# A delta-rule stage on one core: a lag of its own for every stage of a head, a new order of work, and a factor without its masked copy

## The chip, the core and the metric

One core of one Trainium2 chip runs the whole kernel in one launch. Five instruction streams run beside each other and meet at semaphores: TensorE (PE), VectorE (DVE), ScalarE (ACT), GpSimd (POOL) and SyncE (SP), which issues the DMAs. The metric is the device time of one launch in microseconds (us).

## The reference

Two transformer layers over 2 sequences of 512 tokens with 256 channels. The change lies in the first attention, a gated delta rule with 32 value heads of 128 x 128 state, two to each of 16 key heads:

```python
mixed = silu(causal_conv1d(x @ w_qkv, conv_w))   # 4 taps
q, k, v = split(mixed);  q, k = l2norm(q), l2norm(k)
beta = sigmoid(x @ w_b)
g = -exp(A_log) * softplus(x @ w_a + dt_bias)
for t in range(512):                             # per head
    St = St * exp(g_t)
    delta = (v_t - k_t @ St) * beta_t
    St = St + outer(k_t, delta)
    o_t = (q_t * 128**-0.5) @ St
core = rmsnorm(o) * norm_weight * silu(x @ w_z)
x = x + core @ w_out
```

After it come a routed feed-forward layer, a causal attention and a second routed feed-forward layer; these are the same before and after the change.

## The kernel before, in words

`phase_delta` handles one key head at a time (HK = 16 heads; here "head" means that with its two value heads and the two sequences, U = 4 units). The 512 tokens are cut into CH = 4 chunks of 128. Everything is fp32.

A head goes through two groups of stages. The first is the projection: `conv0` to `conv7` (PE), their eviction `conv_r` (ACT, two passes, L807 and L808), the three remaining taps `tapa`, `tapb`, `tapc` (DVE, L943), `silu` (ACT, L819), transposes `queries`, `keys`, `vals`, the gate (`gate` on PE, `gate_r` on ACT), the decay matrices (`row` loads on SP, `gap` on POOL at L733 and L735, `dexp` on ACT at L861), the Gram products (`gram`, `mt`, `at`), the scalars (`scal` copies a head's scalars into `hs`, `nscal` on POOL works out factors such as `nck`), and the factor `nl` (DVE, L990). For `nl`, POOL first writes `cm`, a strictly lower mask times the column `nck` (L741), and DVE multiplies the Gram block by it. The 16 x 16 diagonal blocks of `nl` are then sent through DRAM into lanes (`gath`, `gathr`), inverted there by small DVE operations (`lane0` to `lane12`), transposed (`yl`) and sent back (`putx`, `puty`, `scatx`, `scaty`) into X16 and Y.

The second group (`TURN_STAGES`) merges the inverted blocks to 32, 64 and 128 (`v`, `m`, `y`, `a`, `xa`, `xb`; the number is 2 x level + half), and then walks over the chunks: `recall`, `rhs`, `solve`, `dl`, `ds`, `update`, `st` carry the state, `recallq`, `qs`, `output`, `o` make the output, and `square`, `factor`, `oz`, `corev`, `core`, `core_r`, `project`, `project_r` norm, gate and project it into x.

The order is written out by hand: `WINDOW` is one list of some 230 names, and each engine takes from it, in this order, those stages that are its own. One window handles the second group of head H and the first group of head H + 1. In front stands `PRO` (the first group of head 0 alone), behind 15 windows `LAST` (the second group of head 15 alone). So each stage is either one window ahead or not. At the start of a window SP runs `head`: it waits until PE has filled everything of the window before and loads the weights of head H + 2 (L600) and the output weights of head H + 1 (L603); then come the `row` loads (L636).

Two PSUM banks `pp` are shared by `conv`, `queries`, `keys`, `vals`, `gate`, `core` and `project` in turn: a use waits until the one two before it has been evicted (`fill`, `taken`, `filled`). Lines that the prediction's steps touch: PE `v` L1223 and L1228, `y` L1246 and L1251, `solve` L1283, `update` L1303, `project` L1323, `gate` L1192; ACT `m` of levels 1 and 2 L880 (writes dr_V), `a` of level 1 L886 and L887 (writes dr_Y); DVE `xa` L1089 and L1090, `at` L984, `rhs` L1109; POOL `ds` L760, `am` L748, `oz` L772, `yz` L753 and L754; SP `putx` L653, `scaty` L669, `scatx` L663.

Of the kernel before, what the change touches and what calls it, by code (L numbers as in the profile page):

```python
# [333 lines left out]
WINDOW = """  # L334
conv1 row0 scal conv_r1 row1 conv0 gap0 conv_r0 tapa1 tapb1 tapc1 tapa0 conv3 tapb0 gap1 v0 silu1 conv_r3 m0 row2
tapc0 silu0 conv2 conv_r2 tapa3 dexp0 y0 tapb3 queries0 a0 qsq0 tapc3 xa0 v1 tapa2 v2 dexp1 m2 conv5 y2 row3 m1 y1
yz tapb2 tapc2 silu3 a2 silu2 v4 keys0 xb0 gram0 conv_r5 m4 queries1 keys_r0 ksq0 a1 y4 mt0 v3 gram1 a4 solve0 qsq1
tapa5 keys1 conv4 gap2 tapb5 xa1 mt1 dl0 at0 gap3 m3 ds0 tapc5 y3 keys_r1 at1 update0 ksq1 output0 st0 silu5 gram2
o0 conv_r4 a3 tapa4 recall1 v5 recallq1 dexp2 rhs1 solve1 nscal tapb4 mt2 cm0 xb1 m5 cm1 square0 nl0 tapc4 dl1
dexp3 conv6 gram3 ds1 qs1 mt3 cm2 nl1 y5 update1 silu4 output1 a5 oz0 conv7 st1 cm3 nl2 factor0 conv_r6 nl3 conv_r7  # L340
recall2 gate3 o1 square1 rhs2 solve2 tapa7 gate_r3 vals0 dl2 corev0 ds2 vals1 recallq2 tapa6 vals_r0 tapb6 qs2
tapb7 core0 oz1 gath factor1 vals_r1 update2 output2 tapc6 core_r0 silu6 st2 o2 project0 corev1 square2 gathr lane0
recall3 project_r0 lane1 lane2 recallq3 core1 core_r1 gate0 rhs3 am0 solve3 lane3 lane4 factor2 qs3 lane5 project1
dl3 output3 oz2 lane6 lane7 gate_r0 lane8 corev2 lane9 core2 project_r1 o3 oz3 lane10 gate2 lane11 core_r2 square3
lane12 at2 gate_r2 project2 factor3 corev3 gate1 yl tapc7 putx puty project_r2 vals2 gate_r1 silu7 at3 core3
vals_r2 vals3 am1 vals_r3 core_r3 project3 scaty am2 project_r3 scatx am3
""".split()
# [34 lines left out]


class At:

# [12 lines left out]

def phase_delta(k, sc, w_head_dram, w_out_dram, norm_w_dram):
    nc = k.nc  # L400
    with ExitStack() as ctx:
# [98 lines left out]
        def use(at, name, before=0):  # L500

            if at.kind == "pro":
                return pos_pro[name]
            H = at.H - before
            if isinstance(H, int) and H < 0:
                return pos_pro[name]
            return N_PRO + N_WIN * H + (pos_last if at.kind == "last" and not before else pos_win)[name]

        def on_bank(at, name, before=0):

            n = use(at, name, before)
            return n % NPP, n // NPP

        def run(eng, stages):

            def part(order, i, s, kind):
                at = At(i, s, kind)
                if kind != "pro" and "head" in stages:
                    stages["head"](at)
                for name in order:  # L520
# [5 lines left out]
            part(PRO, None, 0, "pro")
            for H in range(HK - 1):
                part(WINDOW, H // 2, H % 2, "full")
            part(LAST, HK // 2 - 1, 1, "last")
# [6 lines left out]
        def position(at, name):  # L536

            return {"pro": pos_pro, "full": pos_win, "last": pos_last}[at.kind][name]

        def taken(eng, at, names, before=0):  # L540

            order = pos_pro if at.kind == "pro" or before and isinstance(at.H, int) and at.H < before else pos_win
            last = {on_bank(at, n, before)[0]: n for n in sorted(names, key=order.get)}
            for n in last.values():
                b, uses = on_bank(at, n, before)
# [1790 lines left out]
```

## Time and profile before

| | us |
|---|---|
| median of 3 runs | 1684.51 (1678.29 to 1691.55) |
| the profiled execution | 1681.62 |
| its span, first to last instruction | 1679.8 |
| PE busy in the span | 1500.5 (89%) |
| DVE busy | 1203.7 (72%) |
| ACT busy | 877.3 (52%) |
| POOL busy | 894.5 (53%) |

Busy shares are means over stages with different limits. The delta stage runs from about 41 to 1208 us; heads follow one another at the copies of L937, the first window beginning at 106.45 and the drain at 1149.6. A window of one head is therefore the unit in which the change is read. An idle stretch in front of an instruction is printed in brackets with what ended it. A PE group's time includes the end of its last product, so groups that follow each other overlap a little.

### The profile page before, as it was taken

Reading aid. Unit: us, or ns where it says so; the run is one execution under the profiler, and the core shown is the slowest. Engines: PE = TensorE matmul, PEld = TensorE weight load, DVE = VectorE, ACT = ScalarE, POOL = GpSimd, SP = SyncE. Lnnn points to the kernel's source line nnn. Section 1 sums busy time; section 2 is a strip of 40 time slices with the busy share of each in tenths; the row PEclk is TensorE's granted clock in tenths of the full one; section 3 lists DMA queues with packets and bytes.
Section 4 is the critical chain, followed back from the end, with each engine's and each line's share of the span. In section 5 each row is a group of like instructions: output and inputs, shape, how many; then the busy total and the mean of one; then the engine's idle time right before and its main releaser. Section 6 shows DMA issues by size and latency. Waiting matters only on the chain. (4 is left out here: it accounts for less than half of the span.)

```text
span 1679.8 us, 30971 instructions
## 1 busy us (share of the span) xinstructions
PE 1500.5 (89%) x10304; PEld 1057.7 (63%) x10304; DVE 1203.7 (72%) x2693; ACT 877.3 (52%) x2495; POOL 894.5 (53%) x1101
## 2 busy tenths in 40 slices
PE   3679999999999999899999999999899899997897
PEld 3347676676766767667676676767555455555675
DVE  4679788888888988889889897895454355435345
ACT  1547657577585775857758667573311123341121
POOL 0647586686776767767668686683400112122232
PEclk9789999999999999999999999999899978779999
DMA  1120201202112021120220202100021450000413
GB/s 43 70 68 7 63 16 54 68 8 62 18 54 67 8 63 42 33 65 8 62 56 20 63 14 56 40 18 12 1 86 34 160 206 1 1 1 20 139 54 110
DMA packets 128652, 82.73 MB, mean 49 GB/s; under 512 B 92304, under 2 KB 110992, under 8 KB 128368
## 3 DMA queue, kind: packets, MB, share of 16 engines
q1 hardware_dynamic: 125152, 73.52, 15.6%
q0 software_dynamic: 2256, 6.18, 1.0%
q8 instruction: 86, 1.41, 0.3%
q10 hardware_dynamic: 1088, 1.05, 0.2%
q14 instruction: 70, 0.57, 0.1%
HBM read 62.97 MB, written 17.74 MB: 48 GB/s over the span
## 5 line engine op out<-in xcount | busy, mean ns | idle before, releaser
L943 DVE SCALAR_TENSOR_TENSOR dr_acc<-dr_raw,dr_wh,dr_acc 128x512 f32<-128x512 f32 x384 | 353.4, 934 | 46.0 <-ACT dr_acc L808 42.0
L1160 PE MATMUL dr_pp<-xnT,dr_wh 128*128 128x512 f32 x512 | 244.1, 611 | 5.9 <-DMA dr_wh<-in_w_head 5.3
L1160 PEld LDWEIGHTS dr_pp<-xnT,dr_wh 128*128 128x128 f32 x512 | 92.9, 194 | 89.4 <-issue 71.6
L733 POOL TENSOR_TENSOR dr_dT<-dr_rows,dr_hs 128x512 f32<-128x512 f32 x64 | 75.5, 1179 | 136.4 <-issue 121.3
L1192 PE MATMUL dr_pp<-dr_wh,xnT 128*128 128x256 f32 x512 | 124.5, 387 | 12.7 <-DVE x L1140 6.6
L1323 PE MATMUL dr_pp<-dr_wo,xn 128*128 128x256 f32 x512 | 124.6, 387 | 3.6 <-issue 1.8
L807 ACT ACTIVATE dr_raw<-dr_pp 128x512 f32<-128x512 f32 x128 | 76.2, 595 | 93.0 <-PE dr_pp L1160 67.9
L772 POOL TENSOR_TENSOR xn<-xn,dr_zs 128x512 f32<-128x512 f32 x64 | 95.7, 1495 | 43.4 <-DVE xn L1135 32.4
L1192 PEld LDWEIGHTS dr_pp<-dr_wh,xnT 128*128 128x128 f32 x512 | 95.7, 192 | 29.8 <-DVE x L1140 10.1
L1993 POOL TENSOR_SCALAR_AFFINE_SELECT at_pT<-at_pT 128x128 f32<-128x128 f32 x128 | 36.1, 292 | 141.2 <-ACT at_pT L2140 140.1
L760 POOL TENSOR_TENSOR dr_ds<-dr_dl,dr_hs 128x512 f32<-128x512 f32 x48 | 57.0, 1187 | 99.8 <-ACT dr_dl L909 99.8
L1323 PEld LDWEIGHTS dr_pp<-dr_wo,xn 128*128 128x128 f32 x512 | 94.6, 193 | 18.8 <-ACT xn L925 5.4
L917 ACT ACTIVATE xn<-xn 128x128 f32<-128x128 f32 x256 | 75.7, 297 | 51.9 <-DVE xn L1135 35.1
L735 POOL TENSOR_TENSOR dr_dT<-dr_dT,cst 128x512 f32<-128x512 f32 x64 | 91.0, 1422 | 5.0
L748 POOL TENSOR_TENSOR dr_dT<-dr_dT,cst 128x512 f32<-128x512 f32 x64 | 80.8, 1283 | 13.0 <-DVE dr_dT L984 13.0
L2140 ACT ACTIVATE at_pT<-at_u 128x512 f32<-128x512 f32 (+3 forms) x128 | 50.4, 444 | 70.2 <-PE at_u L2058 69.8
L808 ACT ACTIVATE dr_acc<-dr_pp,dr_wh 128x512 f32<-128x512 f32 x128 | 87.1, 680 | 0.0
L181 POOL TENSOR_TENSOR rstd<-ln_in,mhalf 128x8 f32<-128x8 f32 x4 | 6.6, 1645 | 141.6 <-DVE ln_in L164 141.6
L2048 PE MATMUL at_u<-at_kT,at_qT 32*128 32x512 f32 (+3 forms) x256 | 81.4, 566 | 0.2 <-DVE at_mx L2186 0.2
L741 POOL TENSOR_TENSOR dr_cm<-cst,dr_nck 128x512 f32<-128x512 f32 x64 | 79.9, 1259 | 2.6 <-DVE dr_nl L990 1.4
L2186 DVE CUSTOM_DVE_ANT_0 at_u<-at_u,at_mask 128x512 f32<-128x512 f32 (+3 forms) x128 | 61.2, 511 | 27.1 <-PE at_u L2048 26.5
L2058 PE MATMUL at_u<-at_qA,at_kT 32*128 32x256 f32 (+3 forms) x256 | 77.2, 636 | 1.9 <-DVE at_mx L2186 1.7
(297 smaller groups left out, 3835.6 us busy)
## 6 DMA issues: line engine op xcount, KB each, us to landing
dr_rows<-gt_rows SPq DMA_DIRECT2D x64, 256.0 KB, 3.5
dr_wh<-in_w_head SPq DMA_DIRECT2D x16, 776.0 KB, 4.5
ex_w<-in_moe SPq DMA_DIRECT2D x18, 608.0 KB, 11.4
dr_wo<-in_w_out SPq DMA_DIRECT2D x16, 256.0 KB, 4.7
dr_sorted_x<-ex_zero SPq DMA_DIRECT2D x1, 3999.0 KB, 29.2
so_xt<-dr_sorted_x SPq DMA_DIRECT2D x3, 1032.0 KB, 10.7
m_w<-in_moe SPq DMA_DIRECT2D x8, 384.0 KB, 3.1
dr_blocks_l<-dr_nl SPq DMA_DIRECT2D x128, 16.0 KB, 1.7
```

The source lines that it names most:

```text
L735: pool.tensor_tensor(d, d, over(k.c(C_SIGN), 1, U), ALU.mult).then_inc(s_gap, 1)
L741: pool.tensor_tensor(cm[p][:], over(k.c(C_GTP), 1, U), over(nck[s][:, units(c)], 2, P), ALU.mult).then_inc(s_cm[p], 1)
L748: pool.tensor_tensor(d, d, over(k.c(C_LE), 1, U), ALU.mult).then_inc(s_am, 1)
L772: pool.tensor_tensor(core[:].rearrange("p (b v) d -> p b v d", b=B), o[:].rearrange("p (b v) d -> p b v d", b=B), z, ALU.mult).then_inc(s_ ...
L807: act.activation(raw[q][:, TAPS - 1:], flat(ps), ACT.Copy)
L808: act.activation(acc[q][:], flat(ps), ACT.Identity, scale=wh[at.ps][:, tap:tap + 1]).then_inc(free, 1)
L943: dve.scalar_tensor_tensor(acc[q][:], raw[q][:, w:w + S], wh[at.ps][:, col:col + 1], acc[q][:], ALU.mult, ALU.add).then_inc(done[q], 1)
L1160: mm = pe.matmul(flat(ps), wh[at.ps][:, w0:w0 + P], k.xnT[:, kt, b * S:(b + 1) * S], start=(kt == 0), stop=(kt == KT - 1))
L1192: mm = pe.matmul(ps[:, 2 * a:2 * a + 2].rearrange("p a b -> p (a b)"), k.xnT[:, kt, n * P:(n + 1) * P], wh[at.ps][:, w0:w0 + REP * DH], st ...
L1323: mm = pe.matmul(ps[:, 2 * b:2 * b + 2].rearrange("p a b -> p (a b)"), cT[:, REP * b + w], wo[s][:, w], start=(w == 0), stop=(w == REP - 1))
L2048: pe.matmul(ps[:, 0:(qt + 1) * P], qT[Q % 2][rows, t0:t0 + P], kT[Q % 2][rows, b * S:b * S + (qt + 1) * P], start=True, stop=True).then_in ...
L2058: pe.matmul(ps[:, 0:S - kb * P], kT[Q % 2][rows, t0:t0 + P], qA[g % 2][rows, kb * P:], start=True, stop=True).then_inc(s_wt, 1)
```

## The change

Each name in the list now carries its own lag as a number of plus signs: in window w, a stage with lag n works on head w - n. Nothing but the lag decides which head a stage is at; `PRO`, `LAST` and `head` are gone, and the pipeline fills and drains by itself over 16 + 3 windows. Most of the first group has lag 1, most of the second lag 2. `row0`, `row1`, `gap0`, `gap1`, `gap2`, `scal`, `yz` and `conv1` have lag 0 and stand late in the list; `project3` and `project_r3` have lag 3 and stand behind `conv3` and `tapa3`; `am`, `putx`, `scatx` and `scaty` have lag 2. The rest of the list is reordered in places: `xa1` stands behind `at1`, `y3` behind `update0`, `tapc4` and `mt3` before the four `nl`, and the four `nl` stand together. `cm` is gone: `nl` multiplies by the column `nck` broadcast along the row, and the mask, a constant, is gone too. (The upper triangle of `nl` is not read where it would matter: the merges read lower blocks and the lanes lower cells.) `loadw` and `loadwo` replace `head`. `scal` no longer waits for the last `corev` of the head whose scalars it overwrites, but for the last `ds`, `qs` and `st`; `gate_r` waits for `oz` in place of `corev`; `core_r` waits for the `project` before it.

```diff
+ORDER = """
+tapa1+ conv0+ conv_r1+ tapb1+ am0++ conv3+ conv_r0+ tapc1+ project3+++ putx++ tapa0+ silu1+ v0++ tapb0+ am1++ conv_r3+
+tapc0+ conv2+ silu0+ tapa3+ queries0+ project_r3+++ gap3+ dexp0+ y0++ m0++ conv_r2+ v1++ tapb3+ scaty++ tapc3+ qsq0+
+v2++ ds0++ a0++ conv5+ dexp1+ tapa2+ y2++ m2++ xa0++ am2++ y1++ m1++ silu3+ tapb2+ v4++ scatx++ a2++ tapc2+ nscal+
+keys0+ xb0++ silu2+ gram0+ tapa5+ conv_r5+ queries1+ a1++ ds1++ m4++ mt0+ y4++ tapb5+ gram1+ keys_r0+ loadwo++ mt1+
+oz0++ v3++ ksq0+ at0+ solve0++ tapc5+ a4++ at1+ keys1+ am3++ qsq1+ xa1++ conv4+ m3++ st0++ update0++ row2+ tapa4+
+dl0++ factor0++ y3++ o0++ keys_r1+ rhs1++ output0++ tapb4+ ksq1+ recall1++ corev0++ mt2+ gram2+ conv_r4+ xb1++ v5++
+a3++ tapc4+ row3+ ds2++ mt3+ gram3+ dexp2+ nl0+ solve1++ square0++ nl1+ recallq1++ oz1++ nl2+ m5++ conv6+ nl3+ dl1++
+y5++ st1++ factor1++ row0 tapa6+ dexp3+ update1++ o1++ qs1++ output1++ rhs2++ corev1++ conv7+ silu4+ tapb6+ recall2++
+tapa7+ conv_r6+ vals_r0+ gate3+ factor2++ silu5+ tapb7+ gath+ solve2++ tapc6+ a5++ vals0+ vals_r1+ conv_r7+ oz2++
+recallq2++ lane0+ gate_r3+ st2++ vals1+ lane1+ dl2++ core0++ corev2++ lane2+ gathr+ square1++ update2++ o2++ output2++
+lane3+ qs2++ oz3++ project_r0++ project0++ core_r0++ lane4+ recall3++ square2++ lane5+ gate0+ factor3++ rhs3++
+gate_r0+ row1 core1++ lane6+ silu6+ lane7+ recallq3++ corev3++ lane8+ core_r1++ solve3++ lane9+ qs3++ project1++
+project_r1++ gap0 output3++ dl3++ lane10+ o3++ puty+ core2++ core_r2++ lane11+ gate2+ square3++ gap1 lane12+
+project2++ scal gate_r2+ gate1+ project_r2++ yl+ gap2 tapc7+ vals2+ gate_r1+ at2+ loadw+ core3++ at3+ silu7+ vals3+ yz
+vals_r2+ core_r3++ conv1 vals_r3+
 """.split()
+WINDOW = [name.rstrip("+") for name in ORDER]
+LAG = {name.rstrip("+"): name.count("+") for name in ORDER}
...
+def window(w):
+
+    return [(w - LAG[name], name) for name in WINDOW if 0 <= w - LAG[name] < HK]
...
+            def loadw(at):
+
+                if at.H + 2 < HK:
+                    sp.wait_ge(s_full, 1 + max(use(at.H, n) for n in WINDOW if stem(n) in ("conv", "vals", "gate")))
+                    load_w(w_head_dram[at.H + 2:at.H + 3], at.s)
+
+            def loadwo(at):
+
+                if at.H + 1 < HK:
+                    if at.H:
+                        sp.wait_ge(s_full, use(at.H - 1, f"project{CH - 1}") + 1)
+                    load_wo(w_out_dram[at.H + 1:at.H + 2], 1 - at.s)
...
-            def cm_(at, c):
-                s, p = at.ps, c % 2
-                pool.wait_ge(s_scal, at.PH + 1)
-                wait(pool, s_nl[p], 2 * at.PH + c // 2)
-                pool.tensor_tensor(cm[p][:], over(k.c(C_GTP), 1, U), over(nck[s][:, units(c)], 2, P),
-                                   ALU.mult).then_inc(s_cm[p], 1)
-
...
-                wait(act, s_core, CH * at.H)
+                wait(act, s_oz, CH * at.H)
...
             def scal(at):
 
                 s, h = at.ps, at.PH
-                wait(dve, s_core, CH * at.H)
+                wait(dve, s_ds, 3 * at.H)
+                wait(dve, s_qs, U * 3 * at.H)
+                wait(dve, s_st, 3 * at.H)
...
             def nl_(at, c):
-                p = c % 2
                 dve.wait_ge(s_mt, CH * at.PH + c + 1)
-                dve.wait_ge(s_cm[p], 2 * at.PH + c // 2 + 1)
-                dve.tensor_tensor(nl[:, units(c)], nl[:, units(c)], cm[p][:], ALU.mult).then_inc(s_nl[p], 1)
+                dve.wait_ge(s_scal, at.PH + 1)
+                dve.tensor_tensor(nl[:, units(c)], nl[:, units(c)], over(nck[at.ps][:, units(c)], 2, P),
+                                  ALU.mult).then_inc(s_nl[c % 2], 1)
```

In the new list each engine's own order can be read off: SP takes putx, scaty, scatx, loadwo, row2, row3, row0, gath, gathr, row1, puty, loadw; POOL takes am0, am1, gap3, ds0, am2, nscal, ds1, oz0, am3, factor0, corev0 and so on to corev3, then gap0, gap1, gap2, yz.

## Rows read from the trace of the kernel before

**Rows 1.** Windows: us, busy PE, PEld, DVE, ACT, POOL (count), PEclk, DMA share, GB/s
```profile
106.45:1149.60 1043.15, 967.38 (x7740) 719.10 (x7739) 896.01 (x1800) 715.31 (x2085) 747.33 (x840) 0.99 0.17 41
459.36:528.34 68.98, 64.03 (x517) 47.52 (x516) 59.74 (x122) 47.69 (x139) 49.77 (x56) 1.00 0.17 42
```

**Rows 2.** Timeline of PE, window 459.36 to 528.34: start, us, engine, line, [idle before]
```profile
463.80 1.15 PE L1228 MATMUL dr_pI<-dr_Y,dr_nl 128*64 128x64 f32 x32
...
473.79 0.69 PE L1246 MATMUL dr_pI<-dr_V,dr_X 128*64 128x64 f32 x16 [1.66 <-ACT dr_V L880]
...
476.73 0.69 PE L1223 MATMUL dr_pI<-dr_Y,dr_nl 128*64 128x64 f32 x16 [1.32 <-ACT dr_Y L887]
...
484.56 0.69 PE L1246 MATMUL dr_pI<-dr_V,dr_X 128*64 128x64 f32 x16
485.17 1.13 PE L1303 MATMUL dr_pA<-dr_ds,dr_ktok 128*128 128x256 f32 x4
...
502.16 1.13 PE L1283 MATMUL dr_pA<-dr_rhs,dr_Y 128*128 128x128 f32 x8 [0.77 <-DVE dr_rhs L1109]
...
525.70 1.99 PE L1323 MATMUL dr_pp<-dr_wo,xn 128*128 128x256 f32 x8
```

**Rows 3.** Timeline of ACT in the same window: dexp1, the copy for y2, v4's
```profile
472.84 0.63 ACT L861 ACTIVATE dr_dT<-dr_dT 128x512 f32<-128x512 f32 x1 [1.13 <-POOL dr_dT L735]
473.37 0.36 ACT L880 ACTIVATE dr_V<-dr_pI 128x256 f32<-128x256 f32 x1
...
475.85 0.27 ACT L887 ACTIVATE dr_Y<-dr_pI 32x128 f32<-32x128 f32 x1
```

**Rows 4.** Timeline of POOL in the same window: gap0 and ds0
```profile
467.25 1.08 POOL L733 TENSOR_TENSOR dr_dT<-dr_rows,dr_hs 128x512 f32<-128x512 f32 x1 [8.54 <-issue]
...
483.19 1.04 POOL L760 TENSOR_TENSOR dr_ds<-dr_dl,dr_hs 128x512 f32<-128x512 f32 x1 [3.19 <-ACT dr_dl L909]
```

**Rows 5.** Timeline of SP, end of the window: DMA issues, start and us of issue
```profile
523.97 3.76 SPq L669 DMA_DIRECT2D dr_Y<-dr_blocks_y  x8
527.78 1.92 SPq L663 DMA_DIRECT2D dr_X<-dr_blocks_x  x4
529.74 0.45 SPq L600 DMA_DIRECT2D dr_wh<-in_w_head  x1
...
530.76 10.07 SPq L636 DMA_DIRECT2D dr_rows<-gt_rows  x4
```

**Rows 6.** DMA issues of the page: KB each, median us from issue to landing
```profile
dr_rows<-gt_rows SPq DMA_DIRECT2D x64, 256.0 KB, 3.5
dr_wh<-in_w_head SPq DMA_DIRECT2D x16, 776.0 KB, 4.5
...
dr_Y<-dr_blocks_y SPq DMA_DIRECT2D x128, 16.0 KB, 1.9
```

**Rows 7.** Groups of instructions, whole span: busy us, mean ns, idle before
```profile
L943 DVE SCALAR_TENSOR_TENSOR dr_acc<-dr_raw,dr_wh,dr_acc 128x512 f32<-128x512 f32 x384 | 353.4, 934 | 46.0 <-ACT dr_acc L808 42.0
...
L741 POOL TENSOR_TENSOR dr_cm<-cst,dr_nck 128x512 f32<-128x512 f32 x64 | 79.9, 1259 | 2.6 <-DVE dr_nl L990 1.4
```

**Rows 8.** Timeline of DVE in the same window: taps, xa1's last, at1, nl3
```profile
471.76 1.59 DVE L943 SCALAR_TENSOR_TENSOR dr_acc<-dr_raw,dr_wh,dr_acc 128x512 f32<-128x512 f32 x1
...
482.34 0.30 DVE L1090 STREAM_TRANSPOSE dr_X<-dr_Y 32x128 f32<-32x128 f32 x1
...
484.70 0.68 DVE L984 TENSOR_TENSOR dr_dT<-dr_pKQ,dr_dT 128x512 f32<-128x512 f32 x1
...
487.84 0.74 DVE L943 SCALAR_TENSOR_TENSOR dr_acc<-dr_raw,dr_wh,dr_acc 128x512 f32<-128x512 f32 x1
...
499.69 0.69 DVE L990 TENSOR_TENSOR dr_nl<-dr_nl,dr_cm 128x512 f32<-128x512 f32 x1 [1.00 <-POOL dr_cm L741]
```

**Rows 9.** Timeline of ACT in the fill: silu4 of head 0
```profile
84.49 0.63 ACT L819 ACTIVATE dr_vT<-dr_acc 128x512 f32<-128x512 f32 x1 [3.38 <-DVE dr_acc L943]
```

**Rows 10.** Timeline of PE in the fill: the first gates of head 0
```profile
86.46 3.78 PE L1192 MATMUL dr_pp<-dr_wh,xnT 128*128 128x256 f32 x8 [6.02 <-ACT dr_acc L808]
```

More of the change, by code:

```diff
@@ L331, in _ @@
             dve.tensor_tensor(sc[:, :, BETAV, :], sc[:, :, BETA, :], emlo[:], ALU.mult).then_inc(beta_ready, 1)
[L334 to L343, printed above, removed]
@@ L469, in phase_delta @@
                                                                                "at", "am"))
-        s_rows, s_cm, s_nl = ([sem(f"{n}{i}") for i in range(2)] for n in ("rows", "cm", "nl"))
+        s_rows, s_nl = ([sem(f"{n}{i}") for i in range(2)] for n in ("rows", "nl"))
         s_tap, s_acc, s_act = ([sem(f"{n}{i}") for i in range(2)] for n in ("tap", "acc", "act"))
@@ L494, in phase_delta, with use, on_bank @@
         NLANE = sum(LANE_OPS)
-        pos_pro, pos_win, pos_last = bank_uses(PRO), bank_uses(WINDOW), bank_uses(LAST)
-        N_PRO, N_WIN = len(pos_pro), len(pos_win)
         N_ZERO = 13
[L500 to L511, printed above, removed]
+        WINDOWS = range(HK + max(LAG.values()))
+        USE = {}
+        for w in WINDOWS:
+            for what in window(w):
+                if stem(what[1]) in BANK_USERS:
+                    USE[what] = len(USE)
+        def use(h, name):
+            return USE[h, name]
+        def on_bank(h, name):
+            n = use(h, name)
             return n % NPP, n // NPP
         def run(eng, stages):
[L516 to L520, printed above, removed]
+            for w in WINDOWS:
+                for h, name in window(w):
                     f = stages.get(stem(name))
                     if f:
+                        at = At(h, name)
                         digits = name[len(stem(name)):]
                         f(at, int(digits)) if digits else f(at)
[L526 to L529, printed above, removed]
         def wait(eng, s, v):
@@ L534, in wait, with taken @@
                 eng.wait_ge(s, v)
[L536 to L545, printed above, removed]
+        def taken(eng, h, names):
+            last = {}
+            for n in names:
+                b, uses = on_bank(h, n)
+                last[b] = max(uses, last.get(b, 0))
+            for b, uses in last.items():
                 eng.wait_ge(s_free[b], uses + 1)
-        def latest(at, *names):
-            return max(names, key=lambda n: position(at, n))
         def filled(eng, at, name):
-            eng.wait_ge(s_full, use(at, name) + 1)
-            b, _ = on_bank(at, name)
+            eng.wait_ge(s_full, use(at.h, name) + 1)
+            b, _ = on_bank(at.h, name)
             return pp[b], s_free[b]
@@ L670, in scaty @@
                                  blocks[2][j].rearrange("u r j -> r u j")).then_inc(s_Y, 16)
-            run(sp, {"head": head, "row": row, "gath": gath, "gathr": gathr, "putx": putx, "puty": puty, "scatx": scatx,
+            run(sp, {"loadw": loadw, "loadwo": loadwo, "row": row, "gath": gath, "gathr": gathr, "putx": putx, "puty": puty, "scatx": scatx,
                      "scaty": scaty})
@@ L1105, in rhs_ @@
                 dve.wait_ge(s_KS, 3 * at.H + c)
-                taken(dve, at, [f"vals{i}" for i in range(4)], 1)
+                taken(dve, at.h, [f"vals{i}" for i in range(4)])
                 wait(dve, s_D, CH * at.H + c)
@@ L1278, in solve @@
                 else:
-                    taken(pe, at, [f"vals{i}" for i in range(4)], 1)
+                    taken(pe, at.h, [f"vals{i}" for i in range(4)])
                     wait(pe, s_dl, CH * at.H)
@@ L1300, in update @@
                 pe.wait_ge(s_dl, CH * at.H + c + 1)
-                taken(pe, at, [f"keys{b}" for b in range(B)], 1)
+                taken(pe, at.h, [f"keys{b}" for b in range(B)])
                 for b in range(B):
```

86 lines of the change are left out of this document (28 added, 58 removed).

## The prediction

> **What bounds the kernel now.** I read the table of windows first, because the change touches only the delta stage. The stage fills, runs 15 full windows (one head each) in 1043.15 us, that is 69.54 us a head [rows 1], and drains. In the full windows TensorE (PE) is busy for 967.38 us, 64.49 a head, and sits idle for 75.77, which is 5.05 a head; DVE is busy for 59.7 of each 69. The undisturbed window in [rows 1] has 64.03 busy and 4.95 idle, at a granted clock of 1.00. So a new order can win at most what PE waits: about 5 us a head, 76 us in all. The timeline of PE in that window says where: 1.66 us before y2 (L1246, released by ACT's copy of dr_V), 1.32 before v4 (L1223, by ACT's copies into dr_Y), 0.77 before solve2 (L1283, by DVE's rhs) [rows 2]. These three are 3.75; the other 1.20 is in pieces of under 0.5.
>
> The timelines of ACT and POOL tell why y2 waits. The copy for y2 stands in ACT's order behind dexp1, and dexp1 had waited 1.13 us for POOL [rows 3]. It began at 472.84, as POOL's gap1 ended, and that was late because gap0 began only at 467.25, after 8.54 us of idleness [rows 4]. What gap0 waited for is its row transfer: SP issues the rows at 530.76 (461.78 in the window before), after the Y blocks (from 523.97) and the weights (529.74), and rows take a median of 3.5 us to land, weights 4.5 [rows 5, 6]. So a queue on SP sets the first third of the window.
>
> **The change part by part.**
>
> *gap0, gap1 and their rows earlier.* They move to the end of the window before, behind corev3, with rows asked for long ahead. dexp0 and dexp1 then find their input ready. project3 and project_r3 move from before conv1 to behind conv3: same work, but conv1, conv_r1 and the taps start about 1.8 us earlier against the rest of PE (one project group is 1.99 us [rows 2]). Both take time off ACT's chain to the copy for y2: 1.13 of wait plus about 1.8. The copy lasted 0.36 and ended 0.06 before y2 [rows 2, 3]; freed by some 2.9 us it is bounded by v2 alone and ready well before y2's place. y2's 1.66 goes. v4's copies follow y2 on ACT and take four times 0.27, about as long as y1 on PE (32 products, 1.15 for the like group at 463.80 [rows 2]), so of 1.32 some 0.15 stays [rows 3]. Gain: 1.66 + 1.17 = 2.83 a head.
>
> *No masked copy of the factor (cm).* Four POOL instructions a head go, 1.259 us each, 79.9 us in all [rows 7]. POOL is off the path, so this is worth nothing by itself; but nl (DVE) had waited 1.00 us for the last of them, and rhs2, for which solve2 waits, stands right behind nl [rows 2, 8]. With nl needing nscal alone, the 1.00 covers solve2's 0.77. Gain 0.77. nl now multiplies by a broadcast column: no row shows that form from SBUF. Below, a DVE pass of 512 from PSUM costs 0.68 [rows 8]; above, I take the mean 0.934 of the slowed taps [rows 7]. I take today's 0.69 [rows 8], nearest in shape; the upper end adds 4 x 0.24 = 1.0 a head to DVE, which then waits less.
>
> *DVE and POOL in each other's way.* A tap on DVE takes 0.74 us with POOL quiet and 1.59 beside a POOL pass over 512 columns [rows 8]; over all 384 the mean is 0.934 [rows 7]. So taps lose about 0.19 x 24 = 4.7 us a head. Removing four POOL passes helps, and gap0 and gap1 now run where DVE evicts from PSUM or waits for conv_r1. But am0, am1 and gap2 move beside the taps, so of the 4.7 I count no gain. The Trainium skill's page "SBUF — State Buffer" (section "SBUF: two separate sides") says that a DVE instruction with two SBUF inputs and a GpSimd one that reads SBUF lock each other out for the whole instruction. By that rule the new nl (two SBUF inputs still) is as exposed as the old one, and no gain comes of dropping the copied operand; the trace agrees with 0.74 against 1.59 [rows 8].
>
> *xa1 later, y3 later.* xa1 moves behind mt1, at0, tapc5 and at1: old xa1 ended at 482.64, at1 at 485.38, so it comes 2.74 later against DVE's chain [rows 8]. y3 started at 484.56, 1.92 after xa1; it moves behind update0, 1.13 later [rows 2]. Slack 1.92 + 1.13 - 2.74 = 0.3. Three taps in this stretch now meet am0, am1 and gap3, which in the old window had ended before (POOL idles 3.19 before ds0 [rows 4]). One block costs up to 1.59 - 0.74 = 0.85. Bounds: 0 and 3 x 0.85 - 0.3 = 2.2. I take one block: 0.5 lost at y3.
>
> *SP's queue.* loadw now waits for the head's last vals and gate, and putx, scaty and scatx stand behind it; loadwo waits for project3 and row2 stands behind that. Count from the end of vals3: loadw 0.45, putx as much as one scaty (3.76 / 8 = 0.47), eight scaty 3.76, landing 1.9: Y is there at 6.6 us [rows 5, 6]. PE meanwhile has conv1, conv0, conv3 and project3: 525.70 - 68.98 = 456.72 to 463.80, 7.1 us [rows 2]. Slack 0.5; today it is 3.6 (the last of eight goes at 523.97 + 3.76 - 0.47 and lands at about 529.2, and v0 is at 463.80 + 68.98 = 532.8). Cost 0, upper bound among the rivals. row2: scatx (1.92) ends at 6.6, loadwo goes at 7.1, row2 at 7.6, landed at 11 to 12. Behind it on POOL stand gap2, yz, am0, am1 and gap3, about 2.4 each for gap2, yz, the pair of am and gap3, some 10 us, so gap3 ends at 21 to 22. ds0 is wanted at 483.19 - 456.72 = 26.5 today [rows 4], less the 2.8 saved ahead of it: 23.7. Slack about 2; cost 0.
>
> *Waits of scal and gate.* Those of scal on s_ds, s_qs and s_st, of gate_r on s_oz and of silu on vals are on work of a head finished earlier in the same order; behind scal stand project_r2 and two at. Cost 0; what hides them is that a full window lies between; if that cover were gone, PE would stand for about one group of 1.99 us a head [rows 2].
>
> *Fill.* In the first part ACT's silu4 waited 3.38 us, for a tap that stood behind nl0, which waited for cm; PE idled 6.02 before gate behind that [rows 9, 10]. tapc4 now stands before nl, and nl waits for no cm. I take 5 of the 6.02 (bounds 3 and 6). Drain: the same chain of turn stages, 0 (plus or minus 2).
>
> **Sum.** Removed a head: 2.83 + 0.77 = 3.60; added at y3 0.5. That is 3.1, and of 5.05 idle 1.95 stays; 15 x 3.1 = 46.5. Fill 5. The profiled execution took 1681.62 us, 1.82 over its span of 1679.8; 1681.6 - 51.5 = 1630. The median of the runs shown is 1684.51 (1678.29 to 1691.55), so the execution lies within them, and I leave 1630.
>
> **The rivals.**
>
> *All waits go* (for it: no head needs the one before; against: DVE has only 9 of 69 us free). 75.8 + 5: 1601.
>
> *The lock takes the place* (for: am0, am1, gap3 beside taps; against: four POOL passes fewer). y3 waits its bound, 2.2 instead of 0.5, and the upper nl price adds 1.0: 2.7 x 15 = 40: 1670.
>
> *Weights ahead of the Y blocks.* 776 KB now go out on SP's queue right before Y. For it: rows issued behind the weights made gap0 late today [rows 4, 5]; against: Y's own issue takes 3.76 of the 4.5 the weights need. If the blocks move one after another only once the weights have landed: 4.5 + 3.76 + 1.9 = 10.2, v0 3.1 late, 15 x 3.1 = 46: 1676, no change that can be told. The Trainium skill, "DMA: Bandwidth & Descriptors" (the paragraph on HWDGE ordering), says that each DMA engine consumes its descriptors in ring order. By that rule Y cannot overtake the weights, and this rival is what it would lead to at worst.
>
> *Slower: POOL stuck at gap2.* POOL takes its work in order, so a late row2 holds am0, gap3 and ds0, then update0 and all of PE behind it. From 2 us of lateness each further us costs a full us a head. It decides from 2 + 51.5 / 15 = 5.4 us on, where the whole gain is gone; a row2 that lands 7 us later (behind wo, weights and Y) costs 5 x 15 = 75: 1705. For it: gap0's 8.54 idle [rows 4]; against: the median landing of 3.5 [rows 6].
>
> **How the numbers follow.** Chances: the forecast 0.55, with its own range 1612 to 1655 (0.75 to 3.6 us of idle left a head); all waits gone 0.10; the lock 0.15; weights 0.10; POOL stuck 0.10. A measurement of this kernel tells about 1% from no change: below 1668 is faster, above 1701 slower. Faster: 0.55 + 0.10 + half the lock, 0.72. Slower: POOL stuck and the rest of its tail, 0.11. Same: 0.17. Range 1600 to 1684: about 0.05 lies below, 0.15 above.
>
> **What would show it.** Right: no wait of PE on ACT's dr_V copy; dexp1 without a wait on POOL; PE idle near 2 us a head; gap0 and gap1 before the taps; gate in the fill 3 to 6 us earlier. Wrong: PE idle before v0 with DMA dr_Y as releaser (weights), before y3 on DVE's dr_X above 1 us (lock), before update0 on POOL's dr_ds (POOL stuck), or PE's busy time a head above 64.5.

## The result and the profile after

The changed kernel takes 1632.14 us, the median of three runs (1625.64 to 1635.31), where the kernel before takes 1684.51. The ratio is 0.9681, with a 95% interval of 0.9604 to 0.9758. Measured again beside other kernels it was 1628.17 us and 0.9658 (0.9636 to 0.9680). The prediction was 1630 us. As a saving, 51.5 us were forecast; the medians give 52.4 and, measured again, 60.0.

The profiled execution took 1625.64 us, with a span of 1623.9, which is 56.0 us less than the one before. Not all of that is the change's: the stages behind the delta stage, which it does not touch, took 463.8 us at a granted clock of 0.92, where the kernel before had 472.9 at 0.89. In the second profiled execution of the changed kernel they took 472.4 at 0.89. So what follows reads the delta stage alone.

Below, the window table for 14 heads of the changed kernel, from the first v0 to the fifteenth. The columns are those of [rows 1].

```profile
109.23:1040.42 931.19, 885.53 (x7224) 671.24 (x7225) 829.54 (x1681) 665.50 (x1949) 634.82 (x728) 1.00 0.18 43
```

A head takes 931.19 / 14 = 66.51 us, where it took 69.54 [rows 1] and the forecast was 66.44. PE's idle time is (931.19 - 885.53) / 14 = 3.26 a head, against 5.05. So idle time fell by 1.8 and not by the 3.1 of the sum; the other 1.2 came out of PE's busy time, 63.25 against 64.49, for the same products. Some 0.3 of that is TensorE's clock: in the heads where the granted clock was 1.00 throughout (10 of the 14 before, 13 now) PE is busy for 64.02 and 63.14. The first experiment shows what lies behind the lower clock.

The next two views are PE's waits, first of the kernel before over the same 14 heads (112.61 to 1086.22), then of the changed one: the operation and line that waited, the engine, tile and line it waited for, us in all, times, longest.

```profile
PE dr_pI L1246 <- ACT dr_V L880: 28.4, 14, 3.1
PE dr_pI L1223 <- ACT dr_Y L887: 14.6, 13, 1.3
PE dr_pA L1283 <- DVE dr_rhs L1109: 10.8, 14, 0.8
PE dr_pp L1192 <- DVE x L1140: 6.1, 14, 0.5
PE dr_pA L1303 <- POOL dr_ds L760: 5.2, 14, 0.4
```

```profile
PE dr_pA L1226 <- DVE dr_st L1089: 15.2, 14, 1.1
PE dr_pp L1142 <- ACT dr_kq L784: 7.8, 8, 2.2
PE dr_pI L1213 <- DVE dr_X L1057: 7.3, 7, 1.2
PE dr_pp L1278 <- POOL xn L755: 6.4, 14, 0.5
PE dr_pp L1127 <- ACT xn L890: 3.4, 14, 0.2
PE dr_pI L1195 <- DMA dr_Y<-dr_blocks_y: 2.4, 5, 0.8
PE dr_pI L1190 <- ACT dr_Y L852: 2.0, 6, 0.6
```

The first list is y2, v4, solve2, gate1 and an update. All of it is gone but 2.0 us of v4. The second list is new but for that line: recall2 waits for st1 in every head, core3 for POOL in every head, keys0 in eight, y3 in six (1.19 us each; the rest of its line is y2). Now one window of the changed kernel. PE: v0, v4, recall2 and the gate behind it. y2 stands between the first two and does not wait.

```profile
573.89 1.15 PE L1195 MATMUL dr_pI<-dr_Y,dr_nl 128*64 128x64 f32 x32
...
583.69 0.69 PE L1190 MATMUL dr_pI<-dr_Y,dr_nl 128*64 128x64 f32 x16 [0.27 <-ACT dr_Y L852]
...
607.12 1.13 PE L1226 MATMUL dr_pA<-dr_st,dr_kq 128*128 128x256 f32 x4 [1.09 <-DVE dr_st L1089]
608.09 1.89 PE L1159 MATMUL dr_pp<-dr_wh,xnT 128*128 128x256 f32 x8
```

DVE in the same window: seven taps in one go, the four nl, st1.

```profile
570.10 5.23 DVE L910 SCALAR_TENSOR_TENSOR dr_acc<-dr_raw,dr_wh,dr_acc 128x512 f32<-128x512 f32 x7 [2.79 <-ACT dr_acc L771]
...
602.12 3.92 DVE L956 TENSOR_TENSOR dr_nl<-dr_nl,dr_nck 128x512 f32<-128x512 f32 x4
605.96 1.11 DVE L1089 SCALAR_TENSOR_TENSOR dr_st<-dr_st,dr_hs,dr_pA 128x128 f32<-128x128 f32 x4
```

POOL: gap0 at the end of the window before, ds0, and one of the factor passes beside the four nl.

```profile
565.21 1.04 POOL L703 TENSOR_TENSOR dr_dT<-dr_rows,dr_hs 128x512 f32<-128x512 f32 x1
...
590.46 1.53 POOL L723 TENSOR_TENSOR dr_ds<-dr_dl,dr_hs 128x512 f32<-128x512 f32 x1 [2.21 <-ACT dr_dl L874]
...
604.25 0.65 POOL L743 TENSOR_TENSOR dr_f<-dr_ss,dr_rqa 128x4 f32<-128x4 f32 x1
```

gap0 and gap1 are done before the taps begin, where gap0 had started 3.45 us after v0 [rows 4]. The seven taps take 0.75 us each. The four nl take 3.92, with oz0, am3 and the small factor passes running beside them; st1 stands behind, and recall2 pays.

### The profile page after: what moved, and what is told of

It reads as the page before. It is cut to its first block and busy times, and to the rows that moved or that the text cites. A ratio compares the mean times of both kernels' runs of the same rounds, so it can differ in the third digit from the quotient of the medians.

```text
span 1623.9 us, 30859 instructions
## 1 busy us (share of the span) xinstructions
PE 1471.9 (91%) x10304; PEld 1051.6 (65%) x10304; DVE 1192.0 (73%) x2693; ACT 873.8 (54%) x2495; POOL 821.9 (51%) x1037
## 5 line engine op out<-in xcount | busy, mean ns | idle before, releaser
L910 DVE SCALAR_TENSOR_TENSOR dr_acc<-dr_raw,dr_wh,dr_acc 128x512 f32<-128x512 f32 x384 | 330.0, 873 | 60.2 <-ACT dr_acc L771 55.2
L735 POOL TENSOR_TENSOR xn<-xn,dr_zs 128x512 f32<-128x512 f32 x64 | 107.3, 1677 | 51.3 <-DVE xn L1102 41.9
L723 POOL TENSOR_TENSOR dr_ds<-dr_dl,dr_hs 128x512 f32<-128x512 f32 x48 | 52.0, 1083 | 126.7 <-ACT dr_dl L874 126.7
L711 POOL TENSOR_TENSOR dr_dT<-dr_dT,cst 128x512 f32<-128x512 f32 x64 | 94.9, 1492 | 0.0
L705 POOL TENSOR_TENSOR dr_dT<-dr_dT,cst 128x512 f32<-128x512 f32 x64 | 87.6, 1369 | 5.0
L771 ACT ACTIVATE dr_acc<-dr_pp,dr_wh 128x512 f32<-128x512 f32 x128 | 87.1, 681 | 0.0
L821 ACT ACTIVATE dr_zs<-dr_pp 128x512 f32<-128x512 f32 x64 | 37.9, 592 | 89.9 <-PE dr_pp L1159 89.9
L755 POOL TENSOR_TENSOR xn<-xn,dr_fac 128x512 f32<-128x512 f32 x64 | 72.6, 1134 | 6.1
L2013 PE MATMUL at_u<-at_kT,at_qT 32*128 32x512 f32 (+3 forms) x256 | 74.7, 531 | 0.2 <-DVE at_mx L2151 0.2
```

What stands on the lines that cost most here:

```text
L705: pool.tensor_tensor(d, d, over(k.c(C_SIGN), 1, U), ALU.mult).then_inc(s_gap, 1)
L711: pool.tensor_tensor(d, d, over(k.c(C_LE), 1, U), ALU.mult).then_inc(s_am, 1)
L735: pool.tensor_tensor(core[:].rearrange("p (b v) d -> p b v d", b=B), o[:].rearrange("p (b v) d -> p b v d", b=B), z, ALU.mult).then_inc(s_ ...
L771: act.activation(acc[q][:], flat(ps), ACT.Identity, scale=wh[at.ps][:, tap:tap + 1]).then_inc(free, 1)
L910: dve.scalar_tensor_tensor(acc[q][:], raw[q][:, w:w + S], wh[at.ps][:, col:col + 1], acc[q][:], ALU.mult, ALU.add).then_inc(done[q], 1)
L2013: pe.matmul(ps[:, 0:(qt + 1) * P], qT[Q % 2][rows, t0:t0 + P], kT[Q % 2][rows, b * S:b * S + (qt + 1) * P], start=True, stop=True).then_in ...
```

## The experiments

Each kernel is the changed one with the edit shown (pieces of the list of stages), measured against the kernel before on the same chip. Head is the mean of the 14 windows from v0 to v0 in the profiled execution; two executions of the changed kernel gave 66.51 and 66.26, so 0.3 there means little. The last column is the mean of those heads alone in which the granted clock was 1.00 throughout, and their number.

| kernel | us | ratio (95%) | head | at clock 1.00 |
|---|---|---|---|---|
| before | 1684.51 | | 69.54 | 69.14 (10) |
| changed | 1632.14 | 0.9681 (0.9604 to 0.9758) | 66.51 | 66.30 (13) |
| changed, measured again | 1628.17 | 0.9658 (0.9636 to 0.9680) | 66.26 | 66.05 (13) |
| old order in the new frame | 1687.04 | 0.9992 (0.9969 to 1.0016) | 70.13 | 69.25 (7) |
| the same without cm | 1663.31 | 0.9849 (0.9816 to 0.9882) | 68.67 | 67.90 (7) |
| old order, gaps early | 1675.81 | 0.9938 (0.9911 to 0.9965) | 69.12 | 69.12 (14) |
| old order, project3 late | 1696.06 | 1.0058 (1.0028 to 1.0089) | 70.76 | 70.17 (5) |
| all three | 1661.03 | 0.9834 (0.9790 to 0.9878) | 68.28 | 67.96 (11) |
| all three, mask passes later | 1667.26 | 0.9871 (0.9847 to 0.9896) | 68.29 | 68.29 (14) |
| changed, gaps back | 1662.89 | 0.9862 (0.9835 to 0.9889) | 68.26 | 68.26 (14) |
| changed, scal waits for corev | 1685.48 | 0.9993 (0.9969 to 1.0018) | 70.21 | 69.10 (4) |
| changed, weights behind scatx | 1623.53 | 0.9616 (0.9593 to 0.9639) | 65.92 | 65.92 (14) |
| changed, st1 ahead of nl2 | 1632.88 | 0.9685 (0.9646 to 0.9725) | 65.87 | 65.87 (14) |
| changed, four moves | 1622.83 | 0.9611 (0.9583 to 0.9639) | 65.78 | 65.62 (13) |

**The old order in the new frame.** Lags and relaxed waits as changed; the old list, cm with it.

```diff
-tapa1+ conv0+ conv_r1+ tapb1+ am0++ conv3+ conv_r0+ tapc1+ project3+++ putx++ tapa0+ silu1+ v0++ tapb0+ am1++ conv_r3+
...
+loadw++ loadwo++ conv1+ row0+ scal+ conv_r1+ row1+ conv0+ gap0+ conv_r0+ tapa1+ tapb1+ tapc1+ tapa0+ conv3+
+tapb0+ gap1+ v0++ silu1+ conv_r3+ m0++ row2+ tapc0+ silu0+ conv2+ conv_r2+ tapa3+ dexp0+ y0++ tapb3+ queries0+
...
```

> The old order of work, with cm, written with lags (1 for the first group, 2 for the second) and with the new waits and the new loads (both loads at the start of the window, as before). Theory, that the gain comes from where gap, project and cm stand: nothing changes, ratio to before 0.995 to 1.005, PE idle in front of y2 on ACT's dr_V copy still 1.6 us or more in most windows. Rival, that the later waits (scal, gate_r) or the split loads carry the gain: ratio 0.985 or less.

Ratio 0.9992: lags and relaxed waits do nothing while the old order stands. What follows can be set against this kernel.

Its clock has to be seen first. In seven of its 14 heads the granted clock was below 1.00: for part of the head PE ran at 1.2 GHz in place of 2.4. Two heads that follow each other (the columns of [rows 1]), and PE in the second:

```profile
671.12:740.14 69.02, 64.00 (x517) 47.49 (x516) 59.74 (x121) 47.74 (x139) 50.19 (x56) 1.00 0.16 43
740.14:811.91 71.77, 66.51 (x518) 49.60 (x517) 59.90 (x121) 47.96 (x139) 49.91 (x56) 0.95 0.15 35
```

```profile
750.80 0.69 PE L1224 MATMUL dr_pI<-dr_V,dr_X 128*64 128x64 f32 x16 [2.46 <-ACT dr_V L856]
...
755.70 1.91 PE L1181 MATMUL dr_pKQ<-dr_kq 128*128 128x256 f32 x4
...
759.52 1.13 PE L1181 MATMUL dr_pKQ<-dr_kq 128*128 128x256 f32 x4
```

y2 waited 2.46 us, and from then on a Gram group took 1.91 us that takes 1.13 four us later; PE is busy for 2.5 us more in this head. In each of the seven heads the clock fell within 1.3 us of the start of y2, behind a wait of 2.46 to 3.82 us. So a long wait at y2 may cost a head more than its own length; that the wait brings the lower clock about is inferred from this order of events, and not tested by itself. The head that the prediction read has a wait of 1.66 and a clock of 1.00.

**Without cm.**

```diff
-mt2+ cm0+ xb1++ m5++ cm1+ square0++ nl0+
+mt2+ xb1++ m5++ square0++ nl0+
...
```

> x1 without cm: nl multiplies by the broadcast column. Theory: DVE no longer waits for cm, solve2's 0.77 us goes in each of 15 windows and the fill is 5 us shorter: 16.5 us less than x1, ratio to before 0.990. Rival, lock: POOL's four passes fewer free the taps as well, up to 4 x 0.85 us a head, 50 us less, if DVE is what PE waits for. Rival, no gain: y2's wait swallows it, ratio 0.997 or more.

It took 23.7 us less than the old order, where 16.5 were expected. The fill gave 2.4 of it (64.9 to 62.5, from the first convolution to v0), and the heads at clock 1.00 gave 1.35 each, against the 0.77 of the forecast. solve2's wait over the 14 heads (the same view as above):

```profile
PE dr_pA L1251 <- DVE dr_rhs L1077: 2.8, 14, 0.2
```

solve2's 10.8 us became 2.8, and the line of the update on POOL's ds (5.2) is gone: cm had stood ahead of ds1 as well. Taps changed too. The groups of the tap line, whole span, first the old order, then this kernel:

```profile
L921 DVE SCALAR_TENSOR_TENSOR dr_acc<-dr_raw,dr_wh,dr_acc 128x512 f32<-128x512 f32 x384 | 355.9, 940 | 45.9 <-ACT dr_acc L782 41.8
```

```profile
L911 DVE SCALAR_TENSOR_TENSOR dr_acc<-dr_raw,dr_wh,dr_acc 128x512 f32<-128x512 f32 x384 | 332.4, 879 | 45.8 <-ACT dr_acc L772 41.8
```

(940 - 879) x 24 = 1.5 us a head less on DVE. So a POOL pass off the path was not free: it lengthened DVE's. How much of the 1.35 comes of the shorter taps isn't shown; solve2 and the update make 0.94 of it.

**Gaps early.**

```diff
-conv1+ row0+ scal+ conv_r1+ row1+ conv0+ gap0+ conv_r0+
+conv1+ conv_r1+ conv0+ conv_r0+
...
+lane12+ scal at2+ gate_r2+ project2++ factor3++ corev3++ gap0 gap1 gate1+
```

> x1 with row0, row1, scal, gap0 and gap1 one window earlier, at its end (cm kept, project3 where it was). Theory: dexp1 no longer waits for POOL; ACT is still late by its own chain, so y2's wait falls from 1.66 to about 0.5 and v4's stays near 1: 1.2 to 1.7 us a head, 18 to 25 us less than x1, ratio 0.985 to 0.990. Rival, that the rows are the whole cause: 2.8 us a head, 42 us less, ratio 0.975. Rival, that POOL only passes the delay on (am1 to am3 now stand behind gap0 and gap1): nothing.

It gained 11.2 us on the old order; the forecast had 2.83 x 15 = 42 for y2 and v4, with project3 late as well. And at a clock of 1.00 the heads take 69.12 us here and 69.25 there: next to nothing. In the means, 70.13 and 69.12, over half of the difference is PE's busy time (64.86 and 64.31), and no head of this kernel has a lower clock. So what early gaps gained alone lies in the heads with the long waits at y2. PE's waits:

```profile
PE dr_pI L1201 <- DVE dr_Y L1060: 14.4, 13, 1.3
PE dr_pI L1229 <- DVE dr_V L1050: 11.2, 26, 0.8
PE dr_pA L1261 <- DVE dr_rhs L1087: 10.8, 14, 0.8
```

The wait on ACT's copy is off the list, as the forecast said. In its place v2 waits for a0, and y0 and y1 for m0 and m1, all on DVE.

**project3 late.**

```diff
-core_r3++ project3++ scaty+ am2+ project_r3++ scatx+ am3+
+core_r3++ scaty+ am2+ scatx+ am3+
...
+conv3+ project3+++ tapb0+
```

> x1 with project3 and project_r3 moved behind conv3 and tapa3, nothing else. Theory: y2's wait hangs on gap1 and so on the rows, which are issued after project3 has filled no longer but after scatx as before; the front of the window starts 1.8 us earlier and waits 1.8 us longer: 0 to 0.3 us a head, ratio 0.997 to 1.0. Rival, that ACT's own chain sets y2: 1.6 us a head, 25 us less, ratio 0.985.

It lost 9.0 us to the old order, which neither theory had; y2's wait grew from 30.8 us to 40.8:

```profile
PE dr_pI L1224 <- ACT dr_V L856: 40.8, 14, 3.9
```

loadwo waits for this project, and the rows stand behind loadwo on SP. With gap0 still behind its rows, the later project makes the rows later. The move pays only with rows asked for ahead.

**All three.** The three edits above together, in the old order.

> x1 with the three edits together: no cm, row0, row1, scal, gap0 and gap1 one window earlier, project3 behind conv3; the rest of the order as of old. Alone these gave 23 us less, 11 us less and 9 us more than x1. Theory, that gap and project work only together (early gaps leave DVE's taps late, a late project leaves the rows late; together neither): 45 to 55 us less than before, ratio 0.967 to 0.973, and nearly all of the whole change. Rival, additive: 25 us less, ratio 0.985, and the rest of the gain comes from the finer reordering.

It gained 26.5 us on the kernel before, no more than the single effects add up to (23.7 + 11.2 - 9.0 = 25.9). The first theory falls: 26 to 30 us of the change's gain (0.9834 against 0.9681 and 0.9658) lies in the rest of the order. That the times add up is in part the clock's doing: in heads at 1.00 the single edits give 1.35 + 0.13 - 0.92 = 0.56 us, all three 1.29. PE's largest wait was now conv2's on ACT's copy L771. DVE and POOL at the start of a window show why; the row of DVE holds four of five taps, the fifth ends at 658.03.

```profile
PE dr_pp L1127 <- ACT dr_acc L771: 25.9, 13, 2.0
```

```profile
651.62 5.62 DVE L910 SCALAR_TENSOR_TENSOR dr_acc<-dr_raw,dr_wh,dr_acc 128x512 f32<-128x512 f32 x4 [2.56 <-ACT dr_acc L771]
```

```profile
651.41 4.63 POOL L711 TENSOR_TENSOR dr_dT<-dr_dT,cst 128x512 f32<-128x512 f32 x3
```

Four taps took 5.62 us beside the three mask passes, 1.4 each, against 0.75 with POOL quiet.

**All three, with the mask passes later.**

```diff
-core_r3++ scaty+ am2+ scatx+ am3+
+core_r3++ scaty+ scatx+
...
+gap3+ am1++ m3++ ds0++ am2++ tapc5+
...
+oz0++ am3++ conv7+
```

> The order of the run with three parts together (1661.03 us, 0.9834), with one thing moved: POOL's last three passes of the causal mask (L711) go from the start of the window, where they stood behind gap0 and gap1 and beside VectorE's first five taps, to behind gap3, ds0 and oz0 of the same window. Theory A (a two-input pass of VectorE doesn't run beside such a pass of POOL, and that is what the three parts lacked): the five taps take about 3.8 us again and not 6.40, the wait of the convolution on ACT's copy (L771, 1.85 us per head) goes, 15 x 1.85 = 28 us, so 1633 us, ratio 0.967. Theory B (the taps are late for another reason, such as the copies that they read): 1661 us, ratio 0.983, and the wait stays.

The five taps and the waits of PE:

```profile
653.46 3.78 DVE L910 SCALAR_TENSOR_TENSOR dr_acc<-dr_raw,dr_wh,dr_acc 128x512 f32<-128x512 f32 x5 [2.56 <-ACT dr_acc L771]
```

```profile
PE dr_pp L1142 <- ACT dr_kq L784: 12.6, 14, 1.3
PE dr_pA L1226 <- DVE dr_st L1089: 10.5, 14, 0.8
...
PE dr_pA L1250 <- DVE dr_rhs L1076: 6.7, 14, 0.5
```

Both theories miss. The mechanism is as theory A says: five taps in 3.78 us, and conv2's 25.9 us of waiting gone. The time isn't: a head takes 68.29 us as before (at clock 1.00, 68.29 against 67.96). The passes now stand beside the nl and st1, whose readers wait 10.5 and 6.7, and keys0 waits 12.6. Moving POOL's passes moved the wait.

**The changed kernel with its gaps back.**

```diff
-v0++ tapb0+ am1++ conv_r3+
+v0++ tapb0+ am1++ gap0+ gap1+ gap2+ conv_r3+
...
```

(gap0, gap1 and gap2 are gone from the end of the list.)

> The changed kernel with gap0, gap1 and gap2 moved back into the next window, behind am1 and ahead of gap3, all else as it is: the part that the prediction priced highest is undone alone. Theory A (the prediction's: early gaps save the wait of y2 on ACT, 1.66 us, and that of v4, 1.17 us, per full head): the waits return, 15 x 2.83 = 42 us, so 1675 us, ratio 0.994. Theory B (the rest of the new order would have taken most of that wait away by itself, since ACT's work ahead of y2 is also shorter): under 15 us lost, ratio under 0.977. Theory C (the new order counts on the early gaps in more places than those two: am1 and ds0 on POOL come late too): over 60 us lost, ratio over 1.005.

It lost 34.7 us to the changed kernel beside it, 2.3 a head: between theory A's 42 and theory B's 15. The waits that came are not A's. Taps and PE's waits:

```profile
648.71 8.08 DVE L911 SCALAR_TENSOR_TENSOR dr_acc<-dr_raw,dr_wh,dr_acc 128x512 f32<-128x512 f32 x7 [2.79 <-ACT dr_acc L772]
```

```profile
PE dr_pI L1191 <- DVE dr_Y L1050: 14.9, 13, 1.6
PE dr_pp L1128 <- ACT dr_acc L772: 14.4, 13, 1.2
PE dr_pp L1136 <- DVE x L1108: 7.7, 13, 0.6
```

y2 does not wait for ACT's copy even so. The gaps beside the seven taps stretch these from 5.23 to 8.08 us, and what DVE owes to v2 and to the queries, and ACT's copy to conv2, comes late. In this order the early gaps pay by keeping off the taps.

**scal waits for corev again.**

```diff
-                wait(dve, s_ds, 3 * at.H)
-                wait(dve, s_qs, U * 3 * at.H)
-                wait(dve, s_st, 3 * at.H)
+                wait(dve, s_core, CH * at.H)
```

> The changed kernel with scal waiting for the last corev again, as before. Theory of the prediction (the later wait costs and brings nothing by itself): 0. What the trace of the changed kernel says: scal runs 3.5 us ahead of the end of corev3, and DVE has project_r2, tapc7, at2, at3 and vals_r behind it, for whose banks PE waits: 2 to 3.5 us a head, 30 to 50 us more than the changed kernel, ratio to before 0.985 to 1.0.

The whole gain went: 0.9993. DVE's waits, then PE's:

```profile
DVE dr_hs L902 <- POOL xn L755: 47.3, 14, 3.4
```

```profile
PE dr_pp L1147 <- DVE dr_vtok L929: 24.8, 14, 1.8
PE dr_pp L1147 <- DVE x L1105: 22.7, 14, 1.7
```

scal stood 3.4 us a head for POOL, with project_r2 and the reads of vals queued behind it. Of the 3.7 us that a head is longer (70.21 against 66.51), 2.7 is waiting and 1.0 is PE's busy time: the granted clock is below 1.00 in ten of the 14 heads, and in nine of these it fell at the waits for vals. The relaxed wait gives nothing by itself (first experiment), but the order can't do without it.

**Weights behind scatx.**

```diff
-at2+ loadw+ core3++
+at2+ core3++
...
-v4++ scatx++ a2++
+v4++ scatx++ loadw++ a2++
```

> The changed kernel with loadw one window later, behind scatx, so that the weights of 776 KB no longer go out ahead of putx, scaty and scatx. Theory: Y lands on average 0.2 us ahead of v0 in the changed kernel, and the wait is 0.17 us a head: 3 us less than the changed kernel, within its noise (ratio to before 0.965 to 0.969), with Y there 3 us ahead of v0. Rival, that the late Y also brings on the 2.17 us waits of keys0 in four windows: 0.7 us a head, 11 us less, ratio 0.962. Rival, that the weights and then rows are now late: slower.

Y lands in a median of 1.9 us again, where it took 3.2 in the changed kernel, and v0 never waits. First the row of DMA issues of the changed kernel, then of this one:

```profile
dr_Y<-dr_blocks_y SPq DMA_DIRECT2D x128, 16.0 KB, 3.2
```

```profile
dr_Y<-dr_blocks_y SPq DMA_DIRECT2D x128, 16.0 KB, 1.9
```

The ratio is 0.9616 against 0.9681 and 0.9658 for the changed kernel: some 0.5% better, about as much as can be told. That is the first rival's number, but not its way: the long waits of keys0 stay (three of 2.2 us, 6.5 in all), and what went is y3's, 7.1 us, and v0's 2.4.

**st1 ahead of nl2.**

```diff
-nl2+ m5++ conv6+ nl3+ dl1++ y5++ st1++ factor1++
+st1++ nl2+ m5++ conv6+ nl3+ dl1++ y5++ factor1++
```

> The changed kernel with st1 ahead of nl2 on DVE instead of behind nl3. Theory: recall2's wait of 1.09 us a head for st1 goes, and nl2 and nl3 are covered: 15 x 1.09 = 16 us less than the changed kernel, ratio to before 0.958. Rival, that the wait turns up at solve2, for which rhs2 is now as late as before: 0 to 0.5 us a head, ratio 0.963 to 0.968.

No gain that can be told: recall2's 15.2 us became 0.5, and solve2 waits instead.

```profile
PE dr_pA L1250 <- DVE dr_rhs L1076: 11.1, 14, 1.5
```

**Four moves.** The weights and st1 as above, rhs2 ahead of tapa6, o3 ahead of lane10.

```diff
-row0 tapa6+ dexp3+ update1++ o1++ qs1++ output1++ rhs2++
+row0 rhs2++ tapa6+ dexp3+ update1++ o1++ qs1++ output1++
...
-output3++ dl3++ lane10+ o3++ puty+
+output3++ dl3++ o3++ lane10+ puty+
```

> The changed kernel with four moves: loadw behind scatx (as in the run that gave 1623.53 us, 0.9616), st1 ahead of nl2 (recall2's wait of 1.09 us), rhs2 ahead of tapa6 (the 0.79 us that solve2 then waits), and o3 ahead of the lane step behind it (core3's wait of 0.46 us on POOL, and the 0.24 us of the convolution behind it on ACT). Theory A (these waits have nothing behind them at that place): 1.09 + 0.46 + 0.24 = 1.79 us per head less than with the weights' move alone, 15 x 1.79 = 27 us, so 1597 us, ratio 0.946. Theory B (each wait that goes is followed by another within a few us, as when st1 was moved by itself): 1615 to 1624 us, ratio 0.957 to 0.962.

Theory B: 1622.83 us, the same as with the weights' move alone. recall2 still waits for st1 in seven of the 14 heads, 6.1 us in all, and y3 is back with its 1.19 us in seven.

**The changed kernel beside these.**

> The changed kernel as it is, for a comparison on the same chip as the runs beside it: 1632 us, ratio 0.968, as it was. If the ratio lies outside 0.960 to 0.976, chips differ by more than the interval says, and the runs of other sessions can't be set against it.

1628.17 us, 0.9658: as it was.

## Why the prediction came out, step by step

The time, 1632 against 1630, agrees better than its terms do. That is in part luck: the largest term was earned in another way than the one forecast, cm and the order gave more than their price, and new waits at recall2, keys0 and core3, which no term has, took some of it back. Per head:

- **y2 and v4, 2.83 forecast.** Their waits fell from 43.0 to 2.0 us over 14 heads, 2.9 a head: right as a wait. As a gain it was mis-sized: early gaps alone gave 11.2 us (0.75 a head, and 0.13 at clock 1.00), late project3 alone cost 9.0. "Bounded by v2 alone" holds in the changed kernel (in the window shown the copy starts at 580.00, when v2's group ends at 579.96); alone it gave nothing, since v2 and y0 themselves came late, behind DVE. Only inside the new order do the early gaps give 2.3, and that by keeping off the taps. The prediction also took y2's 1.66 from one head; the mean of the 14 was 2.03, and behind the longer waits came the lower clock.
- **cm, 0.77 forecast.** solve2's wait went as described, but the edit alone gave 1.35 a head at clock 1.00. What was missed is ds1 behind cm on POOL (0.37), and DVE's passes that cm held up: of the 4.7 us that taps lose, "I count no gain" was the wrong value, for taps fell from a mean of 934 ns to 873. What that is worth to PE wasn't settled.
- **nl, 0.69 forecast, upper end 0.934.** The price of a pass alone was right and the mean was not. All 64 nl of the changed kernel (line group; the second number is mean ns):

```profile
L956 DVE TENSOR_TENSOR dr_nl<-dr_nl,dr_nck 128x512 f32<-128x512 f32 x64 | 61.2, 1014 | 0.5 <-POOL dr_rqa L694 0.5
```

  The mean of 1014 lies above the range, because the four nl stand beside oz0, am3 and factor0. DVE does not "wait less": st1 behind them became the largest wait, 1.09 a head. That was no part of the sum.
- **y3, a loss of 0.5.** Six waits of 1.19 us in 14 heads, 0.51 a head. The size was right, and so was the mechanism, one block of a tap. But the pass that decides is ds0, which is none of the three that the text named. It comes at almost the same time as the tap ahead of at1 and xa1. First a head in which y3 waits 1.19, then one in which it doesn't:

```profile
258.46 1.04 POOL L723 TENSOR_TENSOR dr_ds<-dr_dl,dr_hs 128x512 f32<-128x512 f32 x1 [1.66 <-ACT dr_dl L874]
258.61 1.45 DVE L910 SCALAR_TENSOR_TENSOR dr_acc<-dr_raw,dr_wh,dr_acc 128x512 f32<-128x512 f32 x1
```

```profile
391.82 0.73 DVE L910 SCALAR_TENSOR_TENSOR dr_acc<-dr_raw,dr_wh,dr_acc 128x512 f32<-128x512 f32 x1
392.00 1.45 POOL L723 TENSOR_TENSOR dr_ds<-dr_dl,dr_hs 128x512 f32<-128x512 f32 x1 [0.30 <-ACT dr_dl L874]
```

  Whichever starts second takes 1.45 us here. Of the 14 heads y3 waits in the six in which this tap took 1.44 us or more, and in no other. With the weights moved alone ds0 never came first, and y3 never waits.
- **SP's queue, slack 0.5.** Y's first block is issued 6.4 us ahead of v0 (567.46 against 573.89 in the window shown) and waits add up to 2.4 us in 14 heads. The order of the rival did come: in all 14 heads the first Y block lands 0.2 to 1.2 us behind the weights. Its size did not: Y's issue had run on meanwhile, so the last block lands 6.8 to 7.9 us after the weights were issued, and not 10.2. In five heads the slack was used up.
- **row2 and POOL, slack 2.** ds0 starts after POOL stood idle for 2.21 us. Right.
- **Waits of scal, 0.** Right for the kernel as changed. Without the cover a head takes 70.21 instead of 66.51, 3.7 us (2.8 at clock 1.00), where the text had 1.99.
- **Fill, 5.** From the first convolution to v0 the changed kernel took 60.4 us and the one before 65.0; PE's wait before the first gate, 6.02 [rows 10], became 1.8. The size was right, the way only half: without cm alone the fill took 62.5, so cm is half of it, but the wait before the gate stayed at 6.13. That wait went with the new order.
- **The order itself, 0 forecast.** The same three edits in the old order gave 0.9834, in the new order 0.9681 and 0.9658. That is 26 to 30 us which the forecast had booked under y2 and v4. The trace shows where part of it is: waits down from 4.09 us a head to 3.26, busy time of PE from 64.20 to 63.25 (63.87 to 63.14 at clock 1.00). So "at most what PE waits" was no bound. The busy time holds hidden waits. In the window above the gate after recall2 starts at 608.09, 0.16 us before recall2's own end of 608.25, and such an overlap of 0.1 to 0.2 us is usual in this window. recall2, which waited, started 1.09 us after the convolution's end: its wait cost 1.25, and 0.16 of it is booked as busy. How much of the 0.7 is of this kind wasn't settled, nor which moves of the rest of the order earn it.

Of the rivals, the lock came in part: 0.51 at y3, and 1.09 at st1, behind nl passes that beside POOL take 3.92 us for four, against the 2.7 that it was given. What went with cm, 1.35, pays for most of that. Of the signs set down, no wait on ACT's copy of dr_V, no wait of dexp on POOL (21.1 us over the 14 heads before), gaps before the taps and the gate 4.0 us earlier (counted from the first convolution) all came; PE idle near 2 us did not (3.26), and y3 did wait above 1 us, in six heads.

## What to carry to other kernels

Cost an instruction on a shared path by what it delays on the other engine, not by whether its own engine is on the critical path: removing passes of a half-idle engine gave 1.35 us a head where the visible wait said 0.77. A wait taken away in a kernel that is 92 to 95% busy is worth little until the order behind it is ready for it, so measure an edit both alone and by taking it back out of the whole. Set heads of the same granted clock against each other, or a gain that belongs to the clock is booked to the stage. A relaxed semaphore can be worth nothing alone and everything in the order that uses it.
